# Context scores from one float32 matmul for a chunk, and the steps of the prologue in another order

## The chip, the cores and the metric

The program runs on one core of a Trainium2 chip. The metric is its time on the device in microseconds. A core has a matmul engine (TensorE, PE in the profile, with its weight loads as PEld), three engines that compute on rows (VectorE is DVE, ScalarE is ACT, GpSimd is POOL) and SyncE (SP), which here only issues transfers. The engines run side by side, each through its own list in its own order, and meet at semaphores.

## What is computed

```python
# x (8, 512, 512), ctx (8, 77, 512), mask (8, 512, 77), all of it float32 but the mask
q = layernorm(x)
s = einsum('bqd,bkd->bqk', q, ctx) / sqrt(512)          # the context scores
p = softmax(where(mask, -1e9, s))
x = x + einsum('bdl,ol->bdo', swap(p @ ctx), W_merge) + b_merge
h = layernorm(x)
rw = gating(h)                                          # weights of 16 experts, 0 for the closed ones
q, k, v = [einsum('bte,bted->btd', rw, einsum('btc,ecd->bted', h, w)) for w in (wq, wk, wv)]
a = softmax(causal(q @ k.T / 8)) @ v
x = x + einsum('bted,edc->btc', a[:, :, None, :] * rw[..., None], w_o)
```

## The kernel before

Work goes by tiles of 128 rows, four to a batch, 32 in all. A tile has eight slots, one for each pair of experts; slot k of a batch is slot g = k % 8 of its tile j. In every slot TensorE makes the q, k and v of two experts (line 1316: twelve matmuls of 384 columns, 400 in slot 0, where the router's 16 columns come along). Three of them stand for one float32 product: the kernel splits its operands into a high part (float32r, made by ScalarE) and a low part (what is left, made by VectorE), and `products` gives high x high, high x low and low x high. Banks psQ0 to psQ3 take the pairs in turn. VectorE adds each pair, weighted, to acc (lines 1015 and 1018), and pair n may start when pair n - 4 is added. Between the pairs stand small jobs at fixed slots, by tables at the top of the file. They take turns in two banks, psT0 and psT1: a job may start when the job two before it has been read (semaphore moved_lo).

The jobs that matter here, for the tile that lies five ahead (X1_LEAD), are the context scores. Slot 2: ScalarE and VectorE make the high and low part of the turned x (XT, loaded by SyncE) in hT (`turned_high`, line 701, and `turned_low`, line 888). Slot 4: TensorE multiplies them with ctxT, which holds high and low part of the centred context side by side (`x1_score`, lines 1242 and 1244), for each of four chunks of 128 features; then VectorE adds both halves of the bank, scales and clips them at the mask's limit, which GpSimd makes (`x1_limit`, lines 915, 917 and 921), and takes the maximum. ctxT is filled from the bank in slots 22 and 23 by `copy_ctx` on ScalarE and `low_ctx` on VectorE. In slot 2 TensorE also makes the next tile's X2 (`sum_x2`), VectorE adds it (line 964) and normalises it in slot 4 (H, line 975), and in slot 6 H is turned (line 1227) and split into hT (lines 696 and 881). Slots 17 to 23 sum G from att and the merge weights, two of whose parts are loaded again for each (merge_hi, merge_lo, line 471).

The first five tiles' scores are made otherwise: one float32 matmul of the whole x and the whole context for a chunk (`x1_whole_score`, line 1256). Four of them stand in the prologue, ahead of slot 0; the fifth in slot 3 of the first tile, with a second copy of the context (ctx_f[1]).

The prologue also splits the qkv weights, one part for each pair of experts: `w_high` on ScalarE (line 720) and `w_low` on VectorE (line 945). ScalarE makes parts 0 to 2, the first hT_hi, the second slice of the context (`slice_high`, line 716), and then parts 3 to 5; 6 and 7 follow in slots 0 and 1 (W_AHEAD). VectorE makes low parts 0 to 3 there and low part k + 4 in slot k.

```python
                        if qkv and is_first(b) and k + 4 < PAIRS:
                            w_low(k + 4)
```

stands in both kernels at the head of VectorE's slot, ahead of the logits and sums of that slot.

Of the kernel before, what the change touches and what calls it, by code (L numbers as in the profile page):

```python
# [24 lines left out]
P = 128  # L25
# [49 lines left out]
W_AHEAD = 6  # L75
# [40 lines left out]
def cross_attention_then_experts_kernel(nc, x, x_t, ctx_in, mask, merge_t, bias, sim, gates, w_qkv, w_o, out):  # L116
# [21 lines left out]
    with whole:  # L138
# [15 lines left out]
        with ExitStack() as under:  # L154
# [33 lines left out]
        ctxT = sb("ctxT", [P, KC, 2, CP], F32R)  # L188
# [61 lines left out]
        ctx_f = [spread[:, 4 + 2 * n:6 + 2 * n, :].rearrange("p a l -> p (a l)")[:, 0:KC * CP].rearrange(  # L250
            "p (c k) -> p c k", c=KC) for n in range(2)]
# [27 lines left out]
        whole_ctx = sem("whole_ctx")  # L279
        xt_hi, xt_lo = sem("xt_hi"), sem("xt_lo")  # L280
# [29 lines left out]
        MOVES, HIS, OWN_STEPS = 24, 14, 4 * (3 + 5) + 4  # L310
# [109 lines left out]
        with nc.Block() as block:  # L420
# [164 lines left out]
            def _(pool):  # L585
# [41 lines left out]
                for n in range(TILES):  # L627
# [41 lines left out]
            def _(act):  # L669
# [8 lines left out]
                def copy_whole_ctx():  # L678
                    for c in (0, 2):
                        act.wait_ge(moved, moves.step())  # L680
                        act.activation(ctx_f[0][:, c:c + 2, 0:C], ctx_bank(psT[moves.bank()]), ACT.Copy
                                       ).then_inc(moved_lo, 1)

                def copy_ctx(chunks=(0, 2), whole=None):
                    for c in chunks:
                        act.wait_ge(moved, moves.step())
                        if whole is not None:
                            act.activation(whole[:, c:c + 2, 0:C], ctx_bank(psT[moves.bank()]), ACT.Copy
                                           ).then_inc(whole_ctx, 1)
                        act.activation(ctxT[:, c:c + 2, 0, 0:C], ctx_bank(psT[moves.bank()]), ACT.Copy  # L690
                                       ).then_inc(moved_hi, 1)
# [5 lines left out]

                def turned_high(t1, p):

                    act.wait_ge(xt_in, 16 * (t1 - X1_LEAD + 1))  # L700
                    act.activation(hT[p][0][:], XT[p][:], ACT.Copy).then_inc(xt_hi, 1)
# [34 lines left out]
                copy_whole_ctx()  # L736
# [22 lines left out]
                act.wait_ge(dve_init, 1)  # L759
                copy_ctx(whole=ctx_f[1])  # L760
# [6 lines left out]
                w_high(1)  # L767
                w_high(2)
                copy_rows(0)
                slice_high(1)  # L770
                for g in range(3, W_AHEAD):
                    w_high(g)

                def body(b, qkv, lead):
                    for k in range(SLOTS):
# [3 lines left out]
                        if qkv and is_first(b) and k + W_AHEAD < PAIRS:  # L779
                            w_high(k + W_AHEAD)  # L780
# [23 lines left out]
                        if cross and g == X1_HIGH_SLOT:  # L804
                            turned_high(t1, p1)
# [21 lines left out]
                        if qkv and k in CTX_T_AT and live(b + 2, B):  # L827
                            copy_ctx(CTX_T_AT[k])
# [38 lines left out]
            def _(dve):  # L867
# [18 lines left out]
                def turned_low(t1, p):  # L886
                    dve.wait_ge(xt_hi, t1 - X1_LEAD + 1)
                    dve.tensor_tensor(hT[p][1][:], XT[p][:], hT[p][0][:].bitcast(F32), ALU.subtract).then_inc(xt_lo, 1)

                def low_ctx(chunks=(0, 2)):  # L890
                    for c in chunks:
                        lo(ctxT[:, c:c + 2, 1, 0:C], None, ctxT[:, c:c + 2, 0, 0:C], ctx_bank)
# [12 lines left out]
                def x1_limit(t1, p):  # L905
# [3 lines left out]
                    if isinstance(t1, int) and t1 < X1_LEAD:  # L909
                        dve.wait_ge(x1_scale_ready, t1 + 1)  # L910
                        dve.wait_ge(limit_ready, t1 + 1)
                        dve.scalar_tensor_tensor(out=sc[p][:], in0=bank[:, 0:C], scalar=x1_scale[p][:, 0:1],
                                                 in1=limit[p][:], op0=ALU.mult, op1=ALU.min).then_inc(moved_lo, 1)
                    else:
                        dve.tensor_copy(sc[p][:], bank[:, CP:CP + C])
                        dve.drain()
                        dve.tensor_tensor(sc[p][:], bank[:, 0:C], sc[p][:], ALU.add).then_inc(moved_lo, 1)
                        dve.drain()
                        dve.wait_ge(x1_scale_ready, t1 + 1)
                        dve.wait_ge(limit_ready, t1 + 1)  # L920
                        dve.scalar_tensor_tensor(out=sc[p][:], in0=sc[p][:], scalar=x1_scale[p][:, 0:1],
                                                 in1=limit[p][:], op0=ALU.mult, op1=ALU.min)
# [98 lines left out]
                dve.memset(ctxT[:].bitcast(F32), 0.0)  # L1021
# [33 lines left out]
                x1_low(3, 3, 1)  # L1055
                dve.wait_ge(sim_rooted, 1)
# [3 lines left out]
                low_ctx()  # L1060
                slice_low(0)
                dve.wait_ge(ld_x[TILES], 32)
                x1_moments(TILES, 0, x_first[TILES])
                G_low(0)
                x2_moved = add_x2(None)
                row_stats(x2_moved)
                w_low(0, 0)
                dve.wait_ge(sim_hi, 1)
                dve.tensor_tensor(simn[1], sim_f, simn[0].bitcast(F32), ALU.subtract).then_inc(sim_lo, 1)
                normalise(0, 0)  # L1070
                w_low(0, 1)
                low_rows(0)
                w_low(1)
                dve.wait_ge(gate_e_made, 1)
                link(dve.tensor_scalar(gate_e, gate_e, 1.0, None, ALU.add))
                link(dve.reciprocal(gate_e, gate_e))
                link(dve.tensor_scalar(neg_sig[:], gate_e, -1.0, None, ALU.mult))
                w_low(2)
                slice_low(1)
                w_low(3)  # L1080

                def body(b, qkv, lead):
                    for k in range(SLOTS):
# [59 lines left out]
                        if cross and g == X1_HIGH_SLOT:  # L1143
                            turned_low(t1, p1)
# [27 lines left out]
                        if qkv and k in CTX_T_AT and live(b + 2, B):  # L1172
                            low_ctx(CTX_T_AT[k])
# [37 lines left out]
            def _(pe):  # L1211
# [18 lines left out]
                def move_ctx(tile, n, chunks=(0, 2)):  # L1230
                    for c in chunks:
                        bank = ctx_bank(next_bank(centred, n + 1, has_high=not (isinstance(n, int) and n == 0)))
# [4 lines left out]
                def x1_score(t1, p):  # L1237

                    bank = next_bank(xt_lo, t1 - X1_LEAD + 1, has_high=False)
                    for c in range(KC):  # L1240
                        high, low = [part[:, c * P:(c + 1) * P] for part in hT[p]]
                        pe.matmul(bank[:, 0:2 * CP], high, ctxT[:, c, :, :].rearrange("p a k -> p (a k)"),
                                  start=(c == 0), stop=False, skip_group_check=True)
                        last = pe.matmul(bank[:, 0:CP], low, ctxT[:, c, 0, :], start=False, stop=(c == KC - 1),
                                         skip_group_check=True)
                    last.then_inc(moved, 1)
# [225 lines left out]
```

## Time and profile before

| | |
|---|---|
| median of three runs | 902.26 us (902.01 to 905.08) |
| the profiled execution | 902.29 us, of which the span is 900.6 |
| TensorE busy | 872.3 us, 97% |
| weight loads busy | 815.8 us, 91% |
| VectorE busy | 637.1 us, 71% |
| ScalarE busy | 224.1 us, 25% |
| GpSimd busy | 127.2 us, 14% |

Busy time of an engine says how much of the span it worked, not whether anyone waited for it. Matmuls overlap: one that is listed with 0.34 us is followed by the next 0.17 to 0.18 us later, so the distance between two starts is the price of one. A float32 matmul shows as two loads and two matmuls. "Idle before" and the waits name what ended an engine's idle time. The granted clock is that of TensorE, 1.00 for 2.4 GHz and 0.50 for 1.2 GHz.

### The profile page before, as it was taken

What the parts mean: (1) busy time and instruction counts of PE and PEld (TensorE: products, weight loads), DVE (VectorE), ACT (ScalarE), POOL (GpSimd) and SP (SyncE); (2) the same over time, 40 slices, a digit from 0 to 9 for tenths busy, and PEclk for the clock granted to TensorE, in tenths of its full rate; (3) what the DMA queues carried; (4) which work ended last, traced back from release to release, by engine and by line L of the source; (5) the groups of instructions that cost most, each with busy time, mean ns of one, the idle gap of its engine ahead of it and who ended that gap; (6) DMA issues with size and microseconds to landing.
All of it is one profiled execution on the core that took longest, in us unless ns stands there. A gap on an engine that the chain in (4) does not pass through costs nothing.

```text
span 900.6 us, 15890 instructions
## 1 busy us (share of the span) xinstructions
PE 872.3 (97%) x4872; PEld 815.8 (91%) x4872; DVE 637.1 (71%) x1946; ACT 224.1 (25%) x567; POOL 127.2 (14%) x335
## 2 busy tenths in 40 slices
PE   6699999999999999999999999999999999999998
PEld 5599999989999899998999899999899989999996
DVE  6788867767586776866768577775767767575674
ACT  5522312213121222212222132222312112121121
POOL 5121111211011110111102011110111201011100
PEclk9779999999999999999999999999999999999999
DMA  9836415053141531416214261234415142040302
GB/s 307 298 120 167 150 49 143 27 156 126 49 131 39 150 120 61 119 47 179 91 51 130 70 185 61 78 91 119 159 38 138 44 131 96 26 107 27 106 25 94
DMA packets 68194, 96.96 MB, mean 108 GB/s; under 512 B 10905, under 2 KB 34105, under 8 KB 67874
## 3 DMA queue, kind: packets, MB, share of 16 engines
q1 hardware_dynamic: 67554, 95.18, 35.7%
q10 hardware_dynamic: 576, 1.05, 0.3%
q8 instruction: 25, 0.41, 0.2%
q14 instruction: 39, 0.32, 0.1%
HBM read 77.07 MB, written 19.14 MB: 107 GB/s over the span
## 4 chain that ended last, share of the span: by engine, by line
issue 66%; PE 20%; POOLq 9%; POOL 3%; DMA 1%; DVE 1%; ACT 0%; DVEq 0%; SPq 0%; ACTq 0%
PE psQ L1316 11%; PE psM L1417 2%; POOLq L617 2%; POOLq L597 2%; PE psO L1417 2%; POOLq L620 2%; PE psQ L1417 1%; POOL limit L600 1%; POOLq L614 1%; POOLq L599 1%; POOLq L622 1%; POOL pow_out L623 1%; POOL pow_tmp L613 1%; DMA merge_lo<-merge_scratch 1%; PE psO L1262 0%
## 5 line engine op out<-in xcount | busy, mean ns | idle before, releaser
L1316 PE MATMUL psQ<-Wqkv_hi,hT_hi 128*128 128x384 f32 (+1 forms) x1024 | 352.2, 344 | 3.9 <-DVE acc L1015 2.5
L1316 PE MATMUL psQ<-Wqkv_lo,hT_hi 128*128 128x384 f32 (+1 forms) x1024 | 347.9, 340 | 0.0
L1316 PE MATMUL psQ<-Wqkv_hi,hT_lo 128*128 128x384 f32 (+1 forms) x1024 | 347.7, 340 | 0.0
L1018 DVE SCALAR_TENSOR_TENSOR acc<-psQ,RW,acc 128x192 f32<-128x192 f32 x448 | 164.7, 411 | 120.7 <-PE psQ L1316 118.8
L1316 PEld LDWEIGHTS psQ<-Wqkv_hi,hT_hi 128*128 128x128 f32 x1024 | 194.1, 190 | 10.3 <-issue 2.6
L1316 PEld LDWEIGHTS psQ<-Wqkv_lo,hT_hi 128*128 128x128 f32 x1024 | 194.3, 190 | 4.6
L1316 PEld LDWEIGHTS psQ<-Wqkv_hi,hT_lo 128*128 128x128 f32 x1024 | 193.9, 189 | 0.0
L612 POOL TENSOR_TENSOR pow_tmp<-b_mv,eps 128x1 f32<-128x1 f32 x32 | 8.1, 254 | 675.1 <-DVE b_mv L971 675.1
L837 ACT ACTIVATE mixedT_hi<-spread 128x512 fp32r<-128x512 f32 x64 | 40.5, 632 | 189.9 <-DVE spread L1192 144.9
L1417 PE MATMUL psO<-Wo_hi,mixedT_hi 128*128 128x512 f32 x120 | 51.6, 430 | 0.2 <-DVE mixedT_lo L1180 0.2
L1417 PE MATMUL psO<-Wo_hi,mixedT_lo 128*128 128x512 f32 x120 | 47.2, 393 | 0.0
L1417 PE MATMUL psM<-Wo_lo,mixedT_hi 128*128 128x512 f32 x120 | 47.1, 392 | 0.0
L1417 PE MATMUL psO<-Wo_lo,mixedT_hi 128*128 128x512 f32 x120 | 47.0, 392 | 0.0
L1417 PE MATMUL psM<-Wo_hi,mixedT_lo 128*128 128x512 f32 x120 | 47.0, 392 | 0.0
L1417 PE MATMUL psM<-Wo_hi,mixedT_hi 128*128 128x512 f32 x120 | 46.9, 391 | 0.0
L1180 DVE TENSOR_TENSOR mixedT_lo<-spread,mixedT_hi 128x512 fp32r<-128x512 f32 x64 | 43.5, 680 | 4.8 <-ACT mixedT_hi L837 4.8
L1192 DVE TENSOR_TENSOR spread<-spread,attT 128x512 f32<-128x512 f32 x64 | 43.6, 681 | 0.3 <-ACT attT L848 0.3
L820 ACT ACTIVATE qkT<-psT 128x256 fp32r<-128x256 f32 x32 | 12.3, 384 | 125.2 <-PE psT L1342 125.2
L851 ACT ACTIVATE gate_exp<-logit,gate_bias 128x16 f32<-128x16 f32 x32 | 9.9, 308 | 112.6 <-DVE gate_bias L987 112.6
L980 DVE SCALAR_TENSOR_TENSOR logit<-psQ,pow_out,neg_sig 128x16 f32<-128x16 f32 x32 | 7.5, 234 | 41.2 <-PE psQ L1316 41.2
L881 DVE TENSOR_TENSOR hT_lo<-psT,hT_hi 128x512 fp32r<-128x512 f32 x32 | 22.1, 692 | 13.1 <-ACT hT_hi L696 13.1
L842 ACT ACTIVATE probs<-psM,neg_mx 128x128 f32<-128x128 f32 (+3 forms) x31 | 16.2, 522 | 56.3 <-DVE neg_mx L1137 56.3
(206 smaller groups left out, 1307.1 us busy)
## 6 DMA issues: line engine op xcount, KB each, us to landing
spread<-gates_scratch SPq DMA_DIRECT2D x30, 512.0 KB, 6.9
X<-in_x SPq DMA_DIRECT2D x32, 256.0 KB, 2.6
x_scratch<-X SPq DMA_DIRECT2D x32, 256.0 KB, 2.0
resid<-x_scratch SPq DMA_DIRECT2D x32, 256.0 KB, 4.6
out<-resid SPq DMA_DIRECT2D x32, 256.0 KB, 2.1
merge_hi<-merge_scratch SPq DMA_DIRECT2D x28, 256.0 KB, 2.9
merge_lo<-merge_scratch SPq DMA_DIRECT2D x28, 256.0 KB, 3.7
XT<-in_x_t SPq DMA_DIRECT2D x27, 256.0 KB, 3.1
```

Source lines behind the costliest of these rows:

```text
L597: pool.drain()
L617: pool.drain()
L620: pool.drain()
L820: act.activation(qkT[:, :, i * P:(i + 1) * P], src, ACT.Copy).then_inc(moved_hi, 1)
L837: act.activation(mixedT[0][:, 2 * (u % 2):2 * (u % 2) + 2, :], spread[:, 2 * u:2 * u + 2, :], ACT.Copy).then_inc(mix_hi, 1)
L842: act.activation(probs[i % 2][:, 0:(i + 1) * P], score_bank(i, ab)[:, 0:(i + 1) * P], ACT.Exp, bias=neg_mx[i % 2][:, 1:2], scale=HEAD_SCAL ...
L881: dve.tensor_tensor(dst, src, dst_hi.bitcast(F32), ALU.subtract).then_inc(moved_lo, 1)
L1018: dve.scalar_tensor_tensor(out=acc[e][:], in0=src, scalar=w, in1=acc[e][:], op0=ALU.mult, op1=ALU.add).then_inc(expert_added, 1)
L1180: dve.tensor_tensor(mixedT[1][:, 2 * (u % 2):2 * (u % 2) + 2, :], spread[:, 2 * u:2 * u + 2, :], mixedT[0][:, 2 * (u % 2):2 * (u % 2) + 2, ...
L1192: dve.tensor_tensor(pair_of, pair_of, attT[:].unsqueeze(1).broadcast_to([P, 2, 2 * P]), ALU.mult).then_inc(mix_made, 1)
L1316: last = pe.matmul(psQ[g % 4][:, 0:first_col(g) + PW], a[:, c * P:(c + 1) * P], w[:, c, E + g * PW - first_col(g):E + (g + 1) * PW], start ...
L1417: last = pe.matmul(project_banks(h, ab)[i][:], a[:, 2 * (u % 2) + c, place(i)], w[:, 2 * u + c, :], start=(u == 0 and c == 0 and n == 0), ...
```

## The change

Five things are done.

1. All scores are float32: `x1_score` serves every tile, with x from XT and ctxT without parts. `turned_high`, `turned_low`, the copy and the addition in `x1_limit` go.
2. ctxT has no low part; in slots 22 and 23 VectorE alone copies it from the bank. In the prologue ScalarE fills it once, where it made a whole copy and a high part before.
3. In the prologue ScalarE makes the high parts 1 to 4 ahead of the first hT_hi, 5 and 6 ahead of the second slice, 7 behind it; nothing is left for slots 0 and 1.
4. VectorE makes the router's constants (neg_sig) ahead of the first slice's low part, the normalised router weights later, and the low parts 0 to 3 earlier.
5. GpSimd's power for the router norms moves behind the limits of the fourth tile.

```diff
-                        if qkv and is_first(b) and k + W_AHEAD < PAIRS:
-                            w_high(k + W_AHEAD)
...
-                    if n == 2:
+                    if n == TILES - 1:
                         pool.wait_ge(sim_floored, 1)
                         pool.tensor_tensor(sim_rn, sim_ss, half_e, ALU.pow).then_inc(sim_rooted, 1)
...
-                act.wait_ge(dve_init, 1)
-                copy_ctx(whole=ctx_f[1])
+                copy_ctx(ctxT)
                 slice_high(0)
                 G_high(0)
                 w_high(0)
                 act.wait_ge(sim_normed, 1)
                 act.activation(simn[0], sim_f, ACT.Copy).then_inc(sim_hi, 1)
                 moves.step()
-                w_high(1)
-                w_high(2)
+                for g in range(1, 5):
+                    w_high(g)
                 copy_rows(0)
+                w_high(5)
+                w_high(6)
                 slice_high(1)
-                for g in range(3, W_AHEAD):
-                    w_high(g)
+                w_high(7)
...
+                def copy_ctx(chunks):
                     for c in chunks:
-                        lo(ctxT[:, c:c + 2, 1, 0:C], None, ctxT[:, c:c + 2, 0, 0:C], ctx_bank)
+                        dve.wait_ge(moved, moves.step())
+                        dve.tensor_copy(ctxT[:, c:c + 2, 0:C], ctx_bank(psT[moves.bank()])).then_inc(moved_lo, 1)
...
-                    else:
-                        dve.tensor_copy(sc[p][:], bank[:, CP:CP + C])
-                        dve.drain()
-                        dve.tensor_tensor(sc[p][:], bank[:, 0:C], sc[p][:], ALU.add).then_inc(moved_lo, 1)
-                        dve.drain()
-                        dve.wait_ge(x1_scale_ready, t1 + 1)
-                        dve.wait_ge(limit_ready, t1 + 1)
-                        dve.scalar_tensor_tensor(out=sc[p][:], in0=sc[p][:], scalar=x1_scale[p][:, 0:1],
-                                                 in1=limit[p][:], op0=ALU.mult, op1=ALU.min)
+                    dve.wait_ge(x1_scale_ready, t1 + 1)
+                    dve.wait_ge(limit_ready, t1 + 1)
+                    dve.scalar_tensor_tensor(out=sc[p][:], in0=bank[:, 0:C], scalar=x1_scale[p][:, 0:1],
+                                             in1=limit[p][:], op0=ALU.mult, op1=ALU.min).then_inc(moved_lo, 1)
...
                 def x1_score(t1, p):
 
-                    bank = next_bank(xt_lo, t1 - X1_LEAD + 1, has_high=False)
+                    if isinstance(t1, int) and t1 < X1_LEAD:
+                        bank = next_bank(ld_xt[t1], 16, has_high=False)
+                        tile = xt_first[t1]
+                    else:
+                        bank = next_bank(xt_in, 16 * (t1 - X1_LEAD + 1), has_high=False)
+                        tile = XT[p][:]
...
+                    keys = ctxT_first if isinstance(t1, int) and t1 < TILES else ctxT
                     for c in range(KC):
-                        high, low = [part[:, c * P:(c + 1) * P] for part in hT[p]]
-                        pe.matmul(bank[:, 0:2 * CP], high, ctxT[:, c, :, :].rearrange("p a k -> p (a k)"),
-                                  start=(c == 0), stop=False, skip_group_check=True)
-                        last = pe.matmul(bank[:, 0:CP], low, ctxT[:, c, 0, :], start=False, stop=(c == KC - 1),
-                                         skip_group_check=True)
+                        last = pe.matmul(bank[:, 0:C], tile[:, c * P:(c + 1) * P], keys[:, c, 0:C],
+                                         start=(c == 0), stop=(c == KC - 1))
                     last.then_inc(moved, 1)
```

How the lists of two engines read now, in the prologue. ScalarE, from the first slice's high part (cs_hi) to the first tile's gates; G_hi belongs to the merge, Wqkv_hi<-W_raw is one high part of the qkv weights for each x, Wqkv_hi<-spread the router's. Before:

```order
L716 ACTIVATE cs_hi<-cs_raw 77x128
L728 ACTIVATE G_hi<-psO 77x512
L720 ACTIVATE Wqkv_hi<-W_raw 128x4x384
L765 ACTIVATE Wqkv_hi<-spread 128x4x16
L720 ACTIVATE Wqkv_hi<-W_raw 128x4x384 x2
L696 ACTIVATE hT_hi<-psT 128x512
L716 ACTIVATE cs_hi<-cs_raw 77x128
L720 ACTIVATE Wqkv_hi<-W_raw 128x4x384 x4
L851 ACTIVATE gate_exp<-logit,gate_bias 128x16
L720 ACTIVATE Wqkv_hi<-W_raw 128x4x384
```

After:

```order
L697 ACTIVATE cs_hi<-cs_raw 77x128
L709 ACTIVATE G_hi<-psO 77x512
L701 ACTIVATE Wqkv_hi<-W_raw 128x4x384
L745 ACTIVATE Wqkv_hi<-spread 128x4x16
L701 ACTIVATE Wqkv_hi<-W_raw 128x4x384 x4
L682 ACTIVATE hT_hi<-psT 128x512
L701 ACTIVATE Wqkv_hi<-W_raw 128x4x384 x2
L697 ACTIVATE cs_hi<-cs_raw 77x128
L701 ACTIVATE Wqkv_hi<-W_raw 128x4x384
L828 ACTIVATE gate_exp<-logit,gate_bias 128x16
```

Two more high parts stand ahead of hT_hi, and two of the four that stood behind the second slice have moved ahead of it.

VectorE, from the first normalised tile H to the first logits (Wqkv_lo<-W_raw is a low part, of 2x384 half of one; cs_lo is the second slice's low part). Before:

```order
L975 TENSOR_SCALAR H<-X,b_mv,pow_out 128x512
L945 TENSOR_TENSOR Wqkv_lo<-W_raw,Wqkv_hi 128x2x384
L881 TENSOR_TENSOR hT_lo<-psT,hT_hi 128x512
L945 TENSOR_TENSOR Wqkv_lo<-W_raw,Wqkv_hi 128x4x384
L1075 TENSOR_SCALAR spread<-spread 128x16
L1076 RECIPROCAL spread<-spread 128x16
L1077 TENSOR_SCALAR neg_sig<-spread 128x16
L945 TENSOR_TENSOR Wqkv_lo<-W_raw,Wqkv_hi 128x4x384
L938 TENSOR_TENSOR cs_lo<-cs_raw,cs_hi 77x128
L945 TENSOR_TENSOR Wqkv_lo<-W_raw,Wqkv_hi 128x4x384 x2
L980 SCALAR_TENSOR_TENSOR logit<-psQ,pow_out,neg_sig 128x16
```

After:

```order
L939 TENSOR_SCALAR H<-X,b_mv,pow_out 128x512
L909 TENSOR_TENSOR Wqkv_lo<-W_raw,Wqkv_hi 128x4x384
L858 TENSOR_TENSOR hT_lo<-psT,hT_hi 128x512
L909 TENSOR_TENSOR Wqkv_lo<-W_raw,Wqkv_hi 128x4x384 x2
L902 TENSOR_TENSOR cs_lo<-cs_raw,cs_hi 77x128
L909 TENSOR_TENSOR Wqkv_lo<-W_raw,Wqkv_hi 128x4x384
L944 SCALAR_TENSOR_TENSOR logit<-psQ,pow_out,neg_sig 128x16
```

Between the second slice and the logits one low part is left of two; the router's constants are gone from here.


## Rows read from the trace of the kernel before

**Rows 1.** Stretches: us, busy us (count) by engine, granted clock, DMA share, GB/s.
```profile
20.70:23.10 2.40, 0.00 (x0) 0.00 (x0) 2.14 (x7) 2.40 (x6) 0.62 (x2) 1.00 1.07 386
...
24.00:34.10 10.10, 4.41 (x15) 3.92 (x15) 7.83 (x13) 2.33 (x3) 3.60 (x7) 0.50 0.88 321
...
42.70:44.40 1.70, 0.00 (x0) 0.00 (x0) 1.42 (x8) 0.13 (x1) 0.00 (x0) 1.00 0.58 222
...
44.50:54.60 10.10, 9.44 (x31) 9.07 (x32) 9.32 (x21) 0.81 (x3) 3.33 (x7) 0.50 0.09 31
...
60.20:900.60 840.40, 830.32 (x4688) 777.76 (x4686) 592.38 (x1832) 196.55 (x511) 107.04 (x288) 1.00 0.34 98
```

**Rows 2.** Waits: who, on whom, us in total, times, longest.
```profile
DVE acc L1018 <- PE psQ L1316: 118.8, 78, 2.9
...
DVE sc L921 <- POOL limit L600: 17.2, 23, 1.9
...
PE psO L1262 <- DMA merge_lo<-merge_scratch: 6.3, 6, 1.6
...
DVE sc L912 <- POOL x_scale L605: 1.1, 1, 1.1
```

**Rows 3.** Groups by line of VectorE and ScalarE: busy us, mean ns, idle before.
```profile
L888 DVE TENSOR_TENSOR hT_lo<-XT,hT_hi 128x512 fp32r<-128x512 f32 x27 | 18.4, 682 | 0.0
...
L701 ACT ACTIVATE hT_hi<-XT 128x512 fp32r<-128x512 f32 x27 | 16.8, 621 | 1.9 <-DMA XT<-in_x_t 1.8
```

**Rows 4.** Timeline of TensorE's weight loads around two scores: start, length in us.
```profile
41.48 1.03 PEld L1256 LDWEIGHTS psT<-spread,spare_wo 128*128 128x128 f32 x8
...
201.29 0.19 PEld L1316 LDWEIGHTS psQ<-Wqkv_hi,hT_lo 128*128 128x128 f32 x1
201.47 0.19 PEld L1242 LDWEIGHTS psT<-ctxT,hT_hi 128*128 128x128 f32 x1
...
202.31 0.19 PEld L1244 LDWEIGHTS psT<-ctxT,hT_lo 128*128 128x128 f32 x1
```

**Rows 5.** Timeline of ScalarE, then of SyncE's queue with the landing of that load.
```profile
29.50 0.60 ACT L696 ACTIVATE hT_hi<-psT 128x512 fp32r<-128x512 f32 x1 [3.76 <-PE psT L1227]
...
34.87 0.31 ACT L716 ACTIVATE cs_hi<-cs_raw 77x128 fp32r<-77x128 f32 x1 [4.77 <-DMA cs_raw<-in_ctx_in]
35.08 5.60 ACT L720 ACTIVATE Wqkv_hi<-W_raw 128x1536 fp32r<-128x1536 f32 x4
...
16.32 2.05 SPq L438 DMA_DIRECT2D W_raw<-in_w_qkv  x1
...
DMA to landing us min/median/max: 11.7/11.7/11.7
```

**Rows 6.** Timeline of VectorE from the second slice to the first sum.
```profile
35.21 0.29 DVE L938 TENSOR_TENSOR cs_lo<-cs_raw,cs_hi 77x128 fp32r<-77x128 f32 x1 [0.35 <-ACT cs_hi L716]
...
36.59 3.43 DVE L945 TENSOR_TENSOR Wqkv_lo<-W_raw,Wqkv_hi 128x1536 fp32r<-128x1536 f32 x2 [1.09 <-ACT Wqkv_hi L720]
...
39.93 0.23 DVE L980 SCALAR_TENSOR_TENSOR logit<-psQ,pow_out,neg_sig 128x16 f32<-128x16 f32 x1
...
44.27 0.74 DVE L1015 TENSOR_SCALAR acc<-psQ,RW 128x192 f32<-128x192 f32 x2
```

**Rows 7.** Timeline of VectorE (two rows), then of TensorE (four rows).
```profile
47.89 0.69 DVE L888 TENSOR_TENSOR hT_lo<-XT,hT_hi 128x512 fp32r<-128x512 f32 x1
...
56.45 0.30 DVE L921 SCALAR_TENSOR_TENSOR sc<-sc,x_scale,limit 128x77 f32<-128x77 f32 x1 [0.46 <-POOL limit L600]
...
30.87 0.70 PE L1316 MATMUL psQ<-Wqkv_hi,hT_hi 128*128 128x400 f32 x1 [1.41 <-DVE hT_lo L881]
...
45.16 0.66 PE L1316 MATMUL psQ<-Wqkv_hi,hT_hi 128*128 128x384 f32 x1 [2.50 <-DVE acc L1015]
...
57.66 0.63 PE L1227 MATMUL psT<-ident,H 128*128 128x128 f32 x4 [0.56 <-DVE H L975]
...
60.22 0.34 PE L1316 MATMUL psQ<-Wqkv_hi,hT_hi 128*128 128x400 f32 x1
```

More of the change, by code:

```diff
@@ L249, in cross_attention_then_experts_kernel @@
         ones_f, causal_f = scratch[1][:, 0:P], scratch[1][:, P:2 * P]
-        ctx_f = [spread[:, 4 + 2 * n:6 + 2 * n, :].rearrange("p a l -> p (a l)")[:, 0:KC * CP].rearrange(
-            "p (c k) -> p c k", c=KC) for n in range(2)]
+        ctxT_first = spread[:, 4:6, :].rearrange("p a l -> p (a l)")[:, 0:KC * CP].rearrange("p (c k) -> p c k", c=KC)
         psQ = [ps(f"psQ{k}") for k in range(4)]
@@ L676, in centre, with copy_ctx @@
                     act.activation(src, src, ACT.Identity, bias=ctx_mean[:, 0:1]).then_inc(centred, 1)
-                def copy_whole_ctx():
+                def copy_ctx(dst):
                     for c in (0, 2):
                         act.wait_ge(moved, moves.step())
[L681 to L691, printed above, removed]
+                        act.activation(dst[:, c:c + 2, 0:C], ctx_bank(psT[moves.bank()]), ACT.Copy).then_inc(moved_lo, 1)
                 def copy_rows(p):
@@ L827, in body @@
                         if qkv and k in CTX_T_AT and live(b + 2, B):
-                            copy_ctx(CTX_T_AT[k])
+                            moves.step()
                         if qkv and k == G_OUT_AT and live(b + 1, B):
@@ L1055, in _ @@
                 x1_low(3, 3, 1)
+                dve.wait_ge(gate_e_made, 1)
+                link(dve.tensor_scalar(gate_e, gate_e, 1.0, None, ALU.add))
+                link(dve.reciprocal(gate_e, gate_e))
+                link(dve.tensor_scalar(neg_sig[:], gate_e, -1.0, None, ALU.mult))
+                moves.step()
+                moves.step()
+                slice_low(0)
+                dve.wait_ge(ld_x[TILES], 32)
+                x1_moments(TILES, 0, x_first[TILES])
                 dve.wait_ge(sim_rooted, 1)
@@ L1231, in move_ctx @@
                     for c in chunks:
-                        bank = ctx_bank(next_bank(centred, n + 1, has_high=not (isinstance(n, int) and n == 0)))
+                        bank = ctx_bank(next_bank(centred, n + 1, has_high=False))
                         for s in range(2):
@@ L1274, in _ @@
                 pe.wait_ge(pool_init, 2)
+                ctx_moved = {}
                 move_ctx(ctx_first[0], 0)
+                ctx_moved[0] = moves.now()
                 for n in range(TILES):
-                    x1_whole_score(n)
+                    x1_score(n, n % 2)
                     if n == 1:
@@ L1288, in _ @@
                         move_ctx(ctx_first[1], 1)
+                        ctx_moved[1] = moves.now()
                 pe.wait_ge(bias_placed, PLACED)
```

57 lines of the change are left out of this document (11 added, 46 removed).

## The prediction

> **What bounds the kernel now.** I read four views: busy time by stretches, the waits, the groups by line, and then the timelines of the first 60 us. The stretches come first [rows 1]: look at TensorE's busy time and at its granted clock in each. From 60.2 us to the end TensorE is busy for 830.3 of 840.4 us at the full clock. The waits [rows 2] say what is missing there: 6.3 us, in six places, are waits of TensorE for the reload of the merge weights (merge_lo). No wait for VectorE, ScalarE or GpSimd above 0.2 us is left behind 60 us. VectorE in its turn waits 118.8 us for qkv sums. So behind 60 us the time is TensorE's own, and VectorE has slack. Before 60 us it is otherwise: there TensorE waits 2.5 us for the first weighted sum (acc, L1015) [rows 7], and its clock stands at the lower level in two stretches of ten microseconds, 24.0:34.1 and 44.5:54.6 [rows 1]. Only this first part can give something to a change that takes work from VectorE and ScalarE.
>
> **The score on TensorE: nothing.** Each of the 27 scores of the old form is four chunks of two matmuls, 156 and 78 columns. The new form is one float32 matmul of 77 columns for a chunk. The trace has that form already, for the fifth tile (L1256), and shows it as two weight loads and two matmuls for each chunk. So both forms are eight weight loads. In the old form the first and the last load start at 201.47 and 202.31, 0.84 us apart. In the float32 form eight loads take 1.03 us with the last one's 0.19, which is 0.84 us again, at the full clock [rows 4]. That is 0.12 us a load. The columns hide behind the loads: a qkv matmul of 384 columns is followed by the next load 0.18 us later, 0.46 ns a column, so the old 234 columns of a chunk are 0.11 us against 0.24 us for its two loads. I take 0 us. The bounds: the instruction behind the float32 score is not seen in this trace without a wait. If the mix of forms cost one more load each time, it would be 27 x 0.12 = 3.2 us. A gain is excluded as long as there are eight loads.
>
> The Trainium skill ("FP8 and Floating Point Precision", TensorE Precision Notes) says that true float32 takes four passes through the array. By columns that is 4 x 77 = 308 against 234 for a chunk, and speaks against the change; the trace shows the loads as the longer part of either form, and by that row the rule costs nothing here.
>
> **VectorE and ScalarE, tile by tile: nothing behind 60 us.** Removed for each of 27 tiles are VectorE's low part of x (0.68 us, 18.4 in all), a copy of the score and an add, and ScalarE's high part of x (0.62 us, 16.8 in all) [rows 3]. All of it behind 60 us lies beside TensorE's 830 us, where VectorE has 118.8 us of slack. Part of it does not even shorten VectorE's list: the clipped score waits for GpSimd's limit, 17.2 us in 23 tiles [rows 2], and with copy and add gone VectorE arrives sooner and waits longer. The context copies go from ScalarE to VectorE in the place of a subtraction of the same shape: nothing. The six waits for merge_lo stay. Their transfers are released by TensorE's own sums in SyncE's queue, where nothing moves.
>
> **The prologue.** Three moves matter.
>
> First, the power of the router norms on GpSimd moves behind the limits of the fourth tile. VectorE waits 1.1 us there for x_scale [rows 2]. At most this goes, and H, the normalised first tile, comes up to a microsecond sooner. It then meets the second point, so I count nothing. The router constants (three operations of 16 columns) take the place of the context's low parts on VectorE there: nothing either.
>
> Second, ScalarE now makes high parts 3 and 4 ahead of the first hT_hi, which starts at 29.50 before [rows 5]. Weight part 4 was issued at 16.32 and landed 11.7 us later, at 28.0; its conversion takes 1.4 us (5.60 us for four), so hT_hi starts at 29.4 to 29.5 again. Gain 0. If that load landed 1 us later, the first qkv matmul would too, and this is the cost of the move at its worst.
>
> Third, and this is the gain: the old order put four high parts behind the second slice of the context, which lands only at 34.87. So VectorE could not start low part 3 before 36.59 [rows 5, 6]. Two low parts (3.43 us) then stood ahead of the first logits at 39.93. In the new order parts 3 to 6 are converted before the slice. Low part 1 is made while VectorE waits for hT_hi; behind hT_hi (ends at 30.1) come hT_lo, 0.7 us, and low parts 2 and 3, 3.4 us, so low part 3 is made by about 34.3. Behind the slice's low part (35.21) only low part 4 is left: 35.4 + 1.7 = 37.1 us for the logits, 2.8 us sooner. The first acc moves from 44.27 to about 41.5. TensorE's fourth pair and the float32 score end 2.50 us before 45.16, at 42.66 [rows 7]; two sums are then added (42.2), and the 2.5 us wait is gone.
>
> What is late next is VectorE. It goes on with two low parts, five sums and the next tile's norm. All of this moves by the 2.8 us, and by a further 0.6 us where the low part of x stood (47.89) [rows 7]. Copy and add at 55.4 save nothing, since the clip at 56.45 waits for the limit. So H, the normalised second tile, comes 3.4 us sooner: TensorE's transposes start at 54.2 instead of 57.66, and the second tile's first qkv matmul at 56.8 instead of 60.22, if the clock is full.
>
> **The clock takes it back.** TensorE now outruns VectorE. Pair 4, 12 matmuls of 0.18 us, runs from 42.7 to 44.8. The score behind it waits for the bank that X's add frees. That add stood right behind the low part of x, at about 48.5; it starts at 45.1 now and ends at 45.8. With 0.85 us for the score and 2.1 us for each of two pairs TensorE stands before the transposes at about 50.9, and H is there at 54.2: 3.3 us idle. In this trace the clock was granted at 1.2 GHz, half of the full level, in 24.0:34.1 and in 44.5:54.6. Ahead of the first fall TensorE did nothing for 2.4 us (20.7:23.1), and ahead of the second it stood from 42.66 on, with the clock still full in 42.7:44.4 [rows 1]. The waits of up to 1.6 us for merge_lo [rows 2] were followed by none: behind 60 us the clock is full. So I expect the fall in the third wait, where the work that follows has no VectorE ahead of it to hide in. What it costs is half of the time that TensorE works at the lower level. The rows give two lengths: from the first qkv matmul at 30.87 to 34.1, 3.2 us, and from 45.16 to 54.6, 9.4 us [rows 1, 7]. Halved: 1.6 and 4.7 us. I take the middle, 3.1 us.
>
> **Sum.** The profiled execution took 902.3 us with a span of 900.6; the median of the three runs is 902.26, the same. 902.3 - 3.4 + 3.1 = 902.0 us. No difference.
>
> **Rivals.**
> - *No fall.* TensorE's wait at 51 to 54 us leaves the clock alone: 902.3 - 3.4 = 898.9. For it: the clock outlasted 1.6 us of waiting in every case. Against: 3.3 us is more than either of the two waits that came ahead of a fall.
> - *A long low stretch,* as the second one of this trace: 902.3 - 3.4 + 4.7 = 903.6.
> - *Slower: the float32 columns show.* If a chunk costs its columns on top of the old time, 74 more columns at 0.46 ns in each of 108 chunks are 3.7 us, on the forecast 905.7. With a long low stretch it is 907.3. It decides as soon as the four passes of a chunk last longer than its two loads, 0.24 us; the rows put them at 0.14. The extra load of above gives nearly the same time. The rule of the Trainium skill cited above ("FP8 and Floating Point Precision", TensorE Precision Notes) would end here if columns, not loads, set the pace.
> - *The reloads land sooner.* If the quieter engines ended the merge_lo waits, 902.0 - 6.3 = 895.7. Nothing in the rows ties those transfers to the removed work.
> - *The chain doesn't move.* Something else holds the first acc at 44.3, and only the 0.6 us of the removed low part is left, without a new wait: 901.7.
>
> **How the numbers follow.** Forecast 0.38, no fall 0.27, long low stretch 0.17, chain unmoved 0.08, columns or extra load 0.06, reloads 0.04. A difference under 0.5% (4.5 us) is about what a measurement of this kernel can't tell from no change. Faster by more than that needs 897.8 or less: the reloads, and a no-fall case with another microsecond found (0.05 of its 0.27), 0.09. Slower needs 906.8: the columns with a long stretch, or something unseen, 0.05. Within: 0.86. The range of 8 in 10 reaches from the no-fall case less a microsecond to the long stretch plus one: 897.9 to 905.0.
>
> **What would show it.** Eight weight loads for a score and no more than 0.9 us from its first matmul to the next qkv matmul (else the columns count). First logits at about 37.1 and first acc at 41.5 (else the chain is wrong). No wait of TensorE for acc, a wait of about 1 us before the sixth tile's score and one of 3 us before the second tile's transposes, and a lower clock in the ten microseconds behind 54. Total time of TensorE behind the second tile's first qkv matmul unchanged at 840 us, less what the low stretch adds. The prediction is wrong if that stretch is absent, if waits of TensorE for VectorE turn up behind 60 us, or if the merge_lo waits change by more than 1 us in sum.

## The result, and the profile after

The changed kernel takes 905.73 us (median of 14 runs) against 902.06 us for the kernel before on the same chips. The ratio is 1.0042, with a 95% interval of 1.0023 to 1.0061. So it is slower, by 2 to 5.5 us, where 902.0 us was forecast and 905.0 was the upper end of the range. The profiled execution took 906.16 us.

The engines' rows and the stretches, from the page of the changed kernel and its table of windows (columns as in [rows 1]):

```profile
PE 874.5 (97%) x4872; PEld 814.3 (90%) x4872; DVE 612.7 (68%) x1862; ACT 208.4 (23%) x526; POOL 127.8 (14%) x335
...
20.70:23.10 2.40, 0.00 (x0) 0.00 (x0) 1.83 (x9) 2.24 (x4) 0.58 (x1) 0.98 1.06 385
23.10:36.60 13.50, 7.30 (x21) 6.11 (x22) 11.25 (x14) 10.55 (x9) 4.55 (x8) 0.50 0.85 304
36.70:53.60 16.90, 14.91 (x90) 14.46 (x89) 14.62 (x40) 1.12 (x4) 4.75 (x10) 1.00 0.42 157
53.80:57.10 3.30, 2.87 (x11) 2.90 (x12) 2.74 (x9) 1.86 (x7) 0.00 (x0) 0.50 0.62 184
58.10:904.20 846.10, 833.58 (x4688) 777.54 (x4686) 570.04 (x1753) 181.14 (x473) 106.62 (x288) 1.00 0.34 97
```

VectorE and ScalarE work 24.4 and 15.7 us less, as they should. The low clock of 44.5:54.6 in [rows 1] has shrunk to 53.8:57.1. Yet the last stretch, from the second tile's first qkv matmul to the end, lasts 846.1 us. It lasted 840.4 before [rows 1]. The time went behind 58 us, where I had counted nothing. The waits say how (who, on whom, us in total, times, longest):

```profile
DVE acc L982 <- PE psQ L1274: 132.0, 98, 3.0
DVE sc L885 <- POOL limit L596: 25.8, 21, 2.4
DVE gate_bias L951 <- issue: 5.2, 3, 1.8
...
PE psT L1189 <- DVE H L939: 8.6, 5, 4.4
PE psO L1217 <- DMA merge_lo<-merge_scratch: 6.5, 7, 1.4
PE psQ L1274 <- DVE hT_lo L858: 2.3, 4, 1.4
```

Beside [rows 2] three things are new. VectorE stands three times ahead of gate_bias for "issue", which means for nothing that the profile shows. TensorE waits five times for H instead of twice, and four times for hT_lo instead of once. VectorE has more slack on average than before, 132 us against 118.8, and is late all the same.

The three stalls stand at one place of the program: the first tile of batches 3, 4 and 5. The batches 2 to 5 are the four turns of the hardware loop (`LOOP = B - 4`), so a stall follows each of the three jumps back and no other entry. VectorE's timeline of the changed kernel behind the first jump, up to the second tile's logits:

```profile
352.04 0.23 DVE L944 SCALAR_TENSOR_TENSOR logit<-psQ,pow_out,neg_sig 128x16 f32<-128x16 f32 x1 [2.17 <-PE psQ L1274]
352.35 0.18 DVE L950 MAX8 top<-logit 128x8 f32<-128x16 f32 x1
354.05 0.15 DVE L951 TENSOR_SCALAR gate_bias<-top 128x1 f32<-128x1 f32 x1 [1.53 <-issue]
...
366.76 0.30 DVE L885 SCALAR_TENSOR_TENSOR sc<-psT,x_scale,limit 128x77 f32<-128x77 f32 x1 [0.99 <-POOL limit L596]
367.15 0.23 DVE L888 TENSOR_REDUCE x_max<-sc 128x1 f32<-128x77 f32 x1
367.31 0.54 DVE L939 TENSOR_SCALAR H<-X,b_mv,pow_out 128x512 f32<-128x512 f32 x1
...
373.93 0.24 DVE L944 SCALAR_TENSOR_TENSOR logit<-psQ,pow_out,neg_sig 128x16 f32<-128x16 f32 x1 [0.36 <-PE psQ L1274]
```

The same place in the kernel before:

```profile
354.01 0.23 DVE L980 SCALAR_TENSOR_TENSOR logit<-psQ,pow_out,neg_sig 128x16 f32<-128x16 f32 x1 [2.13 <-PE psQ L1316]
354.32 0.18 DVE L986 MAX8 top<-logit 128x8 f32<-128x16 f32 x1
354.53 0.15 DVE L987 TENSOR_SCALAR gate_bias<-top 128x1 f32<-128x1 f32 x1
...
374.88 0.23 DVE L980 SCALAR_TENSOR_TENSOR logit<-psQ,pow_out,neg_sig 128x16 f32<-128x16 f32 x1 [0.35 <-PE psQ L1316]
```

The logits follow TensorE's first qkv sum of a tile directly, so the distance between two of them is what TensorE needed for a tile: 21.89 us after, 20.87 before. In the next two turns it is 22.18 and 22.20 against 20.87 each. I call the sum of the three distances the turn time: 62.61 us before, 66.27 after. So the loop turns cost **3.66 us**, which is the size of the whole loss (what the prologue won in this run and what was lost elsewhere nearly cancel; the sum stands behind the steps of the prediction). Behind the first jump one sees where TensorE stood: the transposes of H start 0.68 us behind the matmul ahead of them, where matmuls follow each other by 0.18, and the next tile's first qkv matmul waits 0.29 us for hT_lo.

What does VectorE wait for? The profile lists queues of kind "instruction", by which the engines get their program. Here is one of them in the whole changed kernel, and in the microsecond 352:353, just ahead of and inside the stall:

```profile
q14 instruction: 41, 0.34, 0.1%
...
q14 instruction: 1, 0.01, 1.9%
```

Its packets are of 0.34 MB / 41 = 8 KB. Behind the jump the changed kernel shows three of them (at 349.6, 352.3 and 354.7 us), and the kernel before two in the same seven microseconds. Further on in the turn they come at 377.6, 414.3 and 442.4 us, and from each packet to the next, from 354.7 on, 125, 129 and 123 of VectorE's traced instructions start, drains and register instructions included. So a packet is some 128 instructions. This gave the theory, **A**: VectorE's program comes in pieces of 8 KB. In the changed kernel the piece in which the loop begins ends six instructions behind the loop's head. VectorE runs those six, and then stands until the next piece is there. The edit removed 43 instructions of VectorE ahead of the loop (the head was number 734 of the built program, and is 691 now), and so moved the head towards the end of a piece. That the changed work itself did nothing of this was still to be shown.

### The profile page after: what moved, and what is told of

The parts are those of the page before. It is cut to its first block, busy times and chain, and to the rows that moved or that the text cites. A ratio compares the mean times of both kernels' runs of the same rounds, so it can differ in the third digit from the quotient of the medians.

```text
span 904.2 us, 15694 instructions
## 1 busy us (share of the span) xinstructions
PE 874.5 (97%) x4872; PEld 814.3 (90%) x4872; DVE 612.7 (68%) x1862; ACT 208.4 (23%) x526; POOL 127.8 (14%) x335
## 4 chain that ended last, share of the span: by engine, by line
issue 53%; PE 34%; POOLq 7%; POOL 2%; DMA 2%; DVE 0%; ACT 0%; DVEq 0%; SPq 0%; ACTq 0%
PE psQ L1274 20%; PE psO L1375 4%; PE psM L1375 4%; POOLq L593 2%; POOLq L613 2%; POOLq L616 2%; PE psT L1211 1%; DMA merge_lo<-merge_scratch 1%; PE psQ L1375 1%; PE psO L1217 1%; POOL limit L596 1%; POOLq L610 1%; PE psM L1348 1%; POOLq L595 1%; POOLq L618 1%
```

## The experiments

**The two halves of the change apart.** The first kernel has the float32 scores, with the old order of the prologue:

```diff
-                    if n == TILES - 1:
+                    if n == 2:
                         pool.wait_ge(sim_floored, 1)
...
-                for g in range(1, 5):
-                    w_high(g)
+                w_high(1)
+                w_high(2)
                 copy_rows(0)
```

VectorE's prologue stands likewise in the order of before.

> The first part of the change alone: float32 scores of whole XT and whole context in every batch, the prologue in the order of before. Theory A (loop turns): VectorE's program is fetched in pieces of 8 KB, the profile's instruction queue q14 moves them, and in the changed kernel the first piece after each backward branch of the loop holds only the first six instructions of the loop, so that VectorE stands 1.5 to 1.8 us at gate_bias in the batches 3, 4 and 5, which costs TensorE some 3.6 us in all. This kernel has the same VectorE loop behind the same number of instructions as the changed kernel, so A expects the three stalls ahead of gate_bias, and 902.1 + 3.6 = 905.7 us (904.7 to 906.5). Rival B (the float32 score itself costs TensorE or its readers something in each tile): also some 905.7, since the scores are the same. Rival C (the new order of the prologue costs later what it gave): 902.1. Rival D (no mechanism, the chip's scatter): 902.1 too, and no stall that repeats.

The second is the other half: the kernel before, with its split scores, and in the new order.

> The second part alone: the prologue order of the changed kernel (weight parts 3 and 4 on ScalarE ahead of the second tile's rows, router constants on VectorE, GpSimd's power of the router matrix one tile later), with the scores of before in high and low parts. The loop of VectorE stands where it stood before, 734 instructions into its program. Theory A: no stall ahead of gate_bias, and the prologue's gain stays, which was 2.1 us up to the third tile: 902.1 - 2.1 = 900.0 us (899.0 to 901.5). Rival B (the float32 score costs): 900.0 as well. Rival C (the order of the prologue costs later): 905.7. Rival D: near 902.

Measured: 906.50 us for the scores alone (ratio 1.0050, 1.0028 to 1.0072), 899.68 us for the order alone (0.9977, 0.9955 to 0.9999). VectorE's line of the scores-only kernel from its waits:

```profile
DVE gate_bias L952 <- issue: 5.0, 3, 1.9
```

The order-only kernel has no such line; VectorE's longest "issue" wait in it is 0.4 us. The turn time is 66.1 us for the scores alone and 62.6 for the order alone. So the loss came with the scores and the gain with the order, which rules out rival C (the gain of the order alone is only just clear of nothing). It does not yet tell A from B, a cost of the score itself.

**The same computation, the loop moved.** A drain computes nothing and takes an instruction's place. In the changed kernel 16 of them in batch 1, ahead of the loop, put its head 15 instructions later (the trace has 16 more drains and one semaphore instruction less):

```diff
                         if qkv and g == SLICE_SLOT and live(t + 2, N_TILES):
                             slice_low(t + 2)
+                        if isinstance(b, int) and b == 1:
+                            for _ in range(1 if k < 16 else 0):
+                                dve.drain()
```

> The changed kernel with 15 more VectorE instructions that do nothing (a drain at the end of each of 16 slots of batch 1, ahead of the loop), so that the loop begins 15 instructions later and the end of the 8 KB piece no longer falls six instructions behind its head. Nothing else differs. Theory A: the three stalls of 1.5 to 1.8 us ahead of gate_bias are gone, TensorE's waits for H fall from 8.6 us in 5 to about 5 us in 2, and the time is 905.7 - 3.6 = 902.1 us (901.2 to 903.2). Rivals B and C (a cost of the score or of the order of the prologue): 905.7, with or without the stalls, since computation and order are those of the changed kernel. Rival D: 905.7 if the stalls are an effect and not a cause.

And the other way round, the same edit in the kernel before with `3 if k < 28 else (2 if k == 28 else 0)`:

> The kernel before with 85 more VectorE instructions that do nothing (drains at the ends of 29 slots of batch 1), so that its loop begins at instruction 819, which is 128 instructions (8 KB) behind the 691 of the changed kernel, and so at the same place of an 8 KB piece. Theory A: three stalls of 1.5 to 1.8 us turn up ahead of gate_bias in batches 3, 4 and 5, which the kernel before does not have, and the time rises by about 3.6 us, to 905.7 us (904 to 907; its chain into H is 0.6 us shorter of slack by the two VectorE steps of the split score). All rivals: 902.1 us, no stall.

Measured: 901.00 us for the padded changed kernel (0.9995, 0.9975 to 1.0015), 4.7 us less than without the drains where 3.6 was expected, and 908.06 us for the padded kernel before (1.0059, 1.0039 to 1.0080). VectorE's timeline of the padded changed kernel has no gap, and its line of waits on H is back to two:

```profile
356.22 0.18 DVE L950 MAX8 top<-logit 128x8 f32<-128x16 f32 x1
356.43 0.15 DVE L951 TENSOR_SCALAR gate_bias<-top 128x1 f32<-128x1 f32 x1
...
PE psT L1192 <- DVE H L939: 7.5, 2, 4.4
```

In the padded kernel before the gap has come, at the same instruction, with about the same size:

```profile
354.20 0.18 DVE L986 MAX8 top<-logit 128x8 f32<-128x16 f32 x1
356.09 0.15 DVE L987 TENSOR_SCALAR gate_bias<-top 128x1 f32<-128x1 f32 x1 [1.71 <-issue]
...
DVE gate_bias L987 <- issue: 4.7, 3, 1.7
PE psT L1230 <- DVE H L975: 8.3, 5, 4.3
```

Turn times: 62.4 and 67.1 us. This shows A. Drains took the stalls out of one kernel and put them into the other, and the stalled instruction was the same one when the head stood 128 instructions further on (819 against 691). With the count of instructions for a packet above, this makes a piece of 8 KB 128 instructions. The padded kernel before came out 2.4 us above my 905.7, outside the range that I had given it. The turns explain 4.5 us of its 6.0. The rest I did not track down; its profiled run also had a long wait for a reload (below).

**How far behind the head is far enough?** Five drains at the end of each of 24 slots put the head 15 instructions ahead of the next end of a piece.

> The changed kernel with 119 more VectorE instructions that do nothing (five drains at the end of each of 24 slots of batch 1): the loop begins at instruction 810, 15 ahead of the next end of an 8 KB piece (the changed kernel: 6 ahead of it; the padded one: 119 ahead). The next piece is asked for 2.5 us after that of the head and is of use 1.7 us later, some 4.4 us behind the branch; 15 instructions into the loop VectorE arrives 5 us behind it. Theory A: no stall over 0.5 us, or one of at most 0.5 us, at resid or the first of the gate weights; a time near 902 to 904 us with the drains. A rival that any end of a piece within the first slot costs a full 1.5 us expects three stalls of that size a few instructions behind spare.

Measured: 903.39 us in one run. VectorE's timeline behind the first jump:

```profile
353.57 0.15 DVE L951 TENSOR_SCALAR gate_bias<-top 128x1 f32<-128x1 f32 x1
...
355.30 0.69 DVE L1094 TENSOR_TENSOR resid<-psM,resid 128x512 f32<-128x512 f32 x1 [1.11 <-issue]
```

The stall has moved down the program with the end of the piece, which speaks for A once more. At the three jumps VectorE stands 1.11, 0.65 and 0.84 us ahead of resid, where it stands 0.26 in the kernels without a stall there. So some 0.9, 0.4 and 0.6 us are the stall's, and I expected at most 0.5: I had put VectorE's arrival later than it is. The second packet came at 353.57, and the first instruction behind it started 1.73 us later. In the changed kernel the packet came at 352.31 and gate_bias started 1.74 us later. In all fifteen stalls of the five traces that have them (the changed kernel, the scores alone, the padded kernel before, this one, and the one with normalise first, below) this distance is 1.72 to 1.89 us, wherever the stalled instruction stands. TensorE hardly noticed the shorter stall: the turn time is 63.0 us. The 903.39 us of one run can't say more.

**The score by itself, without the stalls.** The scores-only kernel with the 15 extra instructions:

> The float32 scores alone, the prologue in the order of before, and the 15 VectorE instructions that do nothing ahead of the loop, so that its head stands where the padded changed kernel has it. It is what the first part of the change costs by itself, without the stalls. Theory A (the float32 score is worth nothing on TensorE and the removed work of VectorE and ScalarE nothing either): 902.0 us, as the kernel before (901 to 903.5); the prologue's removed low part of x may give up to 0.6 us. A rival that the score costs its columns or one weight load more in each tile, 3.2 to 3.7 us, expects 905.5.

Measured: 903.02 us (1.0016, 0.9997 to 1.0036), turn time 62.4. Without the drains the same kernel takes 906.50. The float32 score costs nothing that can be told from zero. A cost of 3.2 to 3.7 us in each run lies at or beyond the interval's end (0.36% of 902 is 3.2 us). The traces agree: in the changed kernel a score takes 0.81 us from its first matmul to the matmul behind it:

```profile
46.38 1.01 PE L1211 MATMUL psT<-ctxT,XT 128*128 128x77 f32 x8
47.19 0.42 PE L1274 MATMUL psQ<-Wqkv_hi,hT_hi 128*128 128x384 f32 x1
```

In the kernel before the split form takes the same 0.81 us:

```profile
201.64 0.23 PE L1242 MATMUL psT<-ctxT,hT_hi 128*128 128x156 f32 x1
...
202.45 0.36 PE L1371 MATMUL psM<-qkT 128*128 128x256 f32 x1
```

Behind 60 us each of the 26 scores of either kernel takes 0.80 to 0.81 us. This refutes a cost of the score on TensorE more sharply than the medians do.

**Another cure: shorten the chain.** VectorE's steps ahead of H in the fifth slot are x1_limit, which waits for GpSimd's limit, and then normalise. I turned them round:

```diff
+                        if prepare and g == NORM_SLOT:
+                            normalise(t + 1, 1 - tp)
                         if cross and g == X1_SCORE_SLOT:
                             x1_limit(t1, p1)
...
-                        if prepare and g == NORM_SLOT:
-                            normalise(t + 1, 1 - tp)
```

> The changed kernel with one VectorE step moved: in the fifth slot of each tile normalise (which writes H, for which TensorE waits) stands ahead of x1_limit (which waits for GpSimd's limit and for which nobody waits at once). The loop stands where it stood, so the stalls of VectorE ahead of gate_bias stay, three of 1.5 to 1.8 us. Theory A (the stalls cost because they reach TensorE through H and its turned rows): H comes some 1.5 us sooner within each tile, TensorE's waits for H fall from 8.6 us in 5 to about 6 us in 2, those for hT_lo from 2.3 to 1.4 us, and 905.7 falls by the 3.6 us of the loop turns and by 1 to 1.5 us in the prologue: 901.0 us (899.5 to 903). Rival E (the stalls reach TensorE by another way, the sums of pairs that keep the psQ banks, or the neg_mx step): 904.5 us, the prologue's share alone.

> Both cures: the 15 VectorE instructions ahead of the loop and normalise ahead of x1_limit. Theory A: no stall at the loop turns, and nothing more to win there than by either alone; beside the padded kernel (901.0 measured) only the prologue's 1 to 1.5 us: 899.8 us (898.5 to 901). If the two gains added up (rival E), 901.0 - 3 = 898 us or less.

> The scores of before in high and low parts, the prologue order of the change, and normalise ahead of x1_limit; the loop begins at instruction 734, where no stall was seen. Theory A: beside the order alone (899.7 measured) the prologue's 1 to 1.5 us by the sooner H: 898.5 us (897 to 900). A rival that the float32 score is worth something of its own on VectorE (8 steps less in each batch) expects this kernel slower than the changed kernel with both cures by 1 us or more; A expects the two within 1.5 us of each other, since VectorE has slack outside the loop turns.

Measured: 901.53 us for the changed kernel with normalise first (0.9993, 0.9977 to 1.0009), **898.13 us** with the padding too (0.9956, 0.9938 to 0.9974), and 899.34 us for the old scores with both orders (0.9967, 0.9947 to 0.9987). The first gained the 4 us that I expected, but not where I expected it. Its TensorE waits, and the prologue's transposes behind them:

```profile
PE psT L1189 <- DVE H L939: 5.5, 2, 4.4
PE psQ L1274 <- DVE hT_lo L858: 3.5, 5, 1.4
...
52.57 0.63 PE L1189 MATMUL psT<-ident,H 128*128 128x128 f32 x4 [1.10 <-DVE H L939]
```

The waits for H inside the loop are gone, and waits for hT_lo have taken their place, since VectorE as a whole is still late there. The turn time only falls from 66.3 to 65.5. The largest part of the gain stands in the prologue. The second tile's first qkv matmul starts at 55.9 instead of 58.1, TensorE waits 1.1 us ahead of the transposes instead of 2.6, and no low clock follows. The two spans differ by 4.7 us, of which these places explain 3.0; the other 1.7 us lie in the rest, which scatters by more than that from trace to trace (its numbers stand behind the steps of the prediction). So my expectation for this kernel was right in its sum and wrong in its parts: the stalls reach TensorE by hT_lo as well as by H. With the padding both are cured and the turn time is 62.4 us, as with the padding alone; what normalise first adds there stands in the prologue, where the second tile's first qkv matmul comes at 54.9 us instead of 57.3. The two gains are 4.2 and 4.7 us by themselves and 7.6 together. I had expected 899.8 us, and 898.5 at the least. This is the fastest of the kernels run, 0.44% below the kernel before. The kernel with the old scores (899.34) is 1.2 us slower, less than these intervals can tell from nothing, so the rival that puts it at 1 us or more is neither shown nor refuted.

## Why the prediction was wrong, by its steps

- **The score on TensorE, 0 us: right.** 0.81 us each in both forms, and 903.02 us for the scores alone without the stalls. The rival "the float32 columns show" named 905.7 us, the time that came, and its mechanism is refuted all the same. A chunk takes 0.20 us. By the Trainium skill's rule ("FP8 and Floating Point Precision", TensorE Precision Notes), true float32 takes four passes, and four of 77 columns at 0.46 ns are 0.14 us, an estimate. That is less than a chunk takes, so they don't show here; that the weight loads set the pace instead is argued from these numbers and was not tested.
- **VectorE and ScalarE, "nothing behind 60 us": this step failed.** It asked what the removed work costs or frees, and took 118.8 us of waits [rows 2] for slack that is there everywhere. It did not ask where the removal puts the instructions that stay. Fewer VectorE instructions moved the head of the loop to six ahead of the end of a fetched piece: three stalls of 1.5 to 1.8 us, 5.2 us in all. Slack swallows only a part of each, some 1.0 us at H (a stall of 1.53 us makes the transposes 0.50 us late); the sums, the old batch's y, the scores' maxima and the chain to the next H stand together in the first tile of a batch, and that they are why the slack is no larger there is argued, not tested. Of 5.2 us 3.66 reach TensorE. The prediction had named waits of TensorE for VectorE behind 60 us as a sign of its being wrong, and they came: three for H and three for hT_lo. None of the rows ahead of the prediction shows a stall of this kind.
- **The prologue's gain, 3.4 us: right in its chain.** The slice's low part comes at 35.19, the logits at 37.06 (37.1 forecast), the first acc at 41.40 (41.5), the transposes at 54.23 (54.2):

```profile
37.06 0.22 DVE L944 SCALAR_TENSOR_TENSOR logit<-psQ,pow_out,neg_sig 128x16 f32<-128x16 f32 x1
41.40 0.74 DVE L979 TENSOR_SCALAR acc<-psQ,RW 128x192 f32<-128x192 f32 x2
54.23 1.08 PE L1189 MATMUL psT<-ident,H 128*128 128x128 f32 x4 [2.62 <-DVE H L939]
```

- **GpSimd's power and the router constants, "up to a microsecond sooner, count nothing": not so in this run, and open in general.** The first H comes 1.1 us later, 28.81 instead of 27.68. G_lo starts 0.3 us later, and TensorE's clock had by then fallen: the three matmuls of the first X take 0.63 to 0.76 us where they took 0.39 to 0.47. The low clock lasts from 23.1 to 36.6 us now (first fence) and lasted from 24.0 to 34.1 [rows 1]. The other traces show that the order alone does not decide it. Of the seven with the new order five have H at 28.7 to 29.4 us and 13.7 us of low clock, but the padded changed kernel and the one with both cures, whose programs differ from the changed one's only behind this place, have it at 27.45 and 27.38, a little sooner than before, and 10.2 us of low clock, as the four with the old order. The first of the three matmuls, after and then before:

```profile
23.48 0.76 PE L1226 MATMUL psT<-G_hi,cs_hi 78*128 78x512 f32 x1 [2.83 <-DVE G_lo L921]
```

```profile
23.16 0.47 PE L1271 MATMUL psT<-G_hi,cs_hi 78*128 78x512 f32 x1 [2.49 <-DVE G_lo L957]
```

- **The clock, 3.1 us taken back: the fall came, its size did not, and the reason that I gave for it does not hold.** It came inside the wait that I had named, at 53.7 us, and was over at 57.1. The waits were 2.6 us instead of 3.3, and the wait ahead of the sixth tile's score did not turn up, since TensorE's fourth pair had itself started at 44.2 and not 42.7. Of the 3.4 us gained at the transposes 2.1 were left at the second tile's first qkv matmul (58.12 against 60.22), so the low clock cost 1.3 us. My case against the rival "no fall" was that 3.3 us is more than the waits ahead of the falls before. The order-only kernel waited 3.08 us at the same place, and its clock stayed full to the end of the tile and beyond (granted clock 1.00 in 53:60):

```profile
54.80 0.63 PE L1226 MATMUL psT<-ident,H 128*128 128x128 f32 x4 [3.08 <-DVE H L974]
```

  The scores-only kernel kept the full clock with 2.98 us there, while the clock fell with 2.32 us in the kernel of the 119 more instructions. So the length of one wait did not decide it, and that the fall came as forecast is in part luck.
- **The reloads of merge, unchanged:** 6.5 against 6.3 us in these two runs, but they vary from run to run (below).

In the profiled spans this adds up: 2.1 us won up to the second tile, 3.7 lost at the loop turns, and 2.0 us left for the rest, which makes 904.2 - 900.6. For the 2.0 us I have no cause to show. The same rest (all from the second tile's first qkv matmul to the last one, without the turns) is 748.6 us before and 750.3 after, and in the nine other traces between 746.9 and 753.7. That the turns' loss equals the loss of the medians is therefore in part chance; what is shown is the loss at the turns, and that 15 instructions took it away.

## What to carry to other kernels

An edit that only removes work from an engine with slack can still cost time, because it moves what stays in that engine's program; look behind each jump back of a loop for "issue" waits and for the instruction queue's packets, and if a stall stands there, some instructions ahead of the loop can take it away (fifteen did here). When two halves of a change have opposite signs, run each alone before either is judged. Average slack says nothing about a stall at one place; ask how close the chain from that place to the bottleneck already is.

## What the runs showed of the hardware that I had not expected

- VectorE's program is fetched in pieces of 8 KB, 128 instructions, and fetched again in each turn of the loop (437 traced instructions from one jump's packet to the next, in the changed kernel). Where the loop's head was 6 instructions ahead of the end of a piece it stood for 1.3 to 2.0 us, where 15, for some 0.4 to 0.9 us, and where 91 (the kernel before) or 119 (the padded one), not at all. The two packets behind a jump were 2.4 to 3.2 us apart, and the second was of use 1.7 to 1.9 us after it was seen. That this queue is VectorE's is inferred from that fixed distance and from the counts.
- The waits for the reload of merge_lo at one place of batch 1 were 0.70 to 2.28 us in the eleven traces, and the two of 2.27 and 2.28 us were followed by TensorE's lower clock level. Batch 1, from its first qkv matmul to that of batch 2, then took 111.1 and 111.5 us, against 108.6 in the changed kernel. The sum matmul behind the wait and the stretch 197:201, of the padded changed kernel and then of the scores-only kernel, whose wait was nearly as long and whose clock stayed full:

```profile
198.10 0.52 PE L1220 MATMUL psO<-merge_hi,att_hi 128*78 128x512 f32 x1 [2.28 <-DMA merge_lo<-merge_scratch]
197.00:201.00 4.00, 2.90 (x9) 2.51 (x10) 1.30 (x5) 0.02 (x1) 2.94 (x8) 0.66 0.50 145
```

```profile
198.44 0.42 PE L1218 MATMUL psO<-merge_hi,att_hi 128*78 128x512 f32 x1 [2.19 <-DMA merge_lo<-merge_scratch]
197.00:201.00 4.00, 2.56 (x14) 2.38 (x15) 1.84 (x6) 0.40 (x1) 2.91 (x10) 1.00 0.50 140
```

The padded kernel before had such a wait of 3.06 us at 528 us, and the lower level began within it. But the length of the wait does not decide it here either: at 309 us the padded changed kernel waited 2.27 us for merge_lo with the clock full, and in the scores-only kernel a wait of 1.56 us for the first acc, at 44.3 us, was followed by the lower level. This is likely a part of the scatter between runs of one kernel (898.4 to 906.7 us for the kernel before); I did not test it. What sets how long a reload takes stays open.
